# The layer norm's negated mean on VectorE instead of GpSimd, in a fused window-attention kernel

## What is computed

```
def ln(x, g, b):
    m = jnp.mean(x, -1, keepdims=True)
    v = jnp.mean(jnp.square(x - m), -1, keepdims=True)
    return (x - m) * jax.lax.rsqrt(v + LN_EPS) * g + b
...
q = ln(q.reshape(B_, E, L).transpose(0, 2, 1), gq, bq)     # k and v alike
attn = jax.nn.softmax(jnp.einsum('bhqd,bhkd->bhqk', q * SCALE, k) + bias[None], axis=-1)
out = jnp.einsum('bhqk,bhkd->bhqd', attn, v)
```

## Time and profile before

| | |
|---|---|
| Median of 3 runs | 852.89 us (851.65 to 853.03) |
| The profiled execution | 853.24 us, its span 851.1 us, 2.1 us outside the span |
| Mean granted clock of TensorE | 0.984 |
| Busy: TensorE / VectorE / ScalarE / GpSimd | 761.1 / 660.4 / 605.7 / 483.2 us |
| Group norm and weights, before the first head | 0 to about 35 us |
| Attention part of one image with its head | about 155 us |
| From one image to the next | about 204 us |

### The profile page before, as it was taken

How to read it: one execution, slowest core, us unless ns; L and a number is a source line. 1 busy time by engine, 2 the same in 40 slices (tenths; PEclk the granted TensorE clock), 3 DMA queues, 4 the chain that set the end, 5 groups by cost and what they waited for, 6 DMA issues and landing times.

```text
span 851.1 us, 19126 instructions
## 1 busy us (share of the span) xinstructions
PE 761.1 (89%) x5704; PEld 537.6 (63%) x5704; DVE 660.4 (78%) x2142; ACT 605.7 (71%) x1287; POOL 483.2 (57%) x1041
## 2 busy tenths in 40 slices
PE   0479999999788999999888999999989899999988
PEld 0347777766356777767445777776735677777753
DVE  6558888878657888878675888887866788888575
ACT  1498888765478888876457888877556888886651
POOL 5468677752237777764144776776233677776410
PEclk9999999999999999999999999999999999999999
DMA  7110123000231030300052013110014212000004
GB/s 250 56 29 30 48 108 106 1 1 1 87 125 55 28 128 0 106 1 2 1 166 70 29 30 126 52 55 1 1 56 137 64 34 78 0 1 2 1 1 148
DMA packets 17655, 47.14 MB, mean 55 GB/s; under 512 B 2080, under 2 KB 2720, under 8 KB 17568
## 3 DMA queue, kind: packets, MB, share of 16 engines
q1 hardware_dynamic: 17568, 46.09, 16.6%
HBM read 37.69 MB, written 8.39 MB: 54 GB/s over the span
## 4 chain that ended last, share of the span: by engine, by line
PE 44%; issue 19%; DVE 16%; POOL 11%; ACT 8%; DVEq 1%; DMA 0%; SPq 0%; ACTq 0%; POOLq 0%
PE y_ps L998 12%; PE o_ps L1065 7%; PE pt_ps L1055 5%; PE s_ps L1044 5%; POOL ln_rs L715 4%; PE s_ps L1087 4%; DVE ln_st L540 3%; ACT qk_n L840 3%; PE ox_ps L1014 3%; PE y_ps L969 2%; ACT sc L855 2%; PE t_ps L1023 2%; ACT v_bd L848 2%; DVE h_hi L509 2%; PE y_ps L993 1%
## 5 line engine op out<-in xcount | busy, mean ns | idle before, releaser
L840 ACT ACTIVATE qk_n<-y_ps,ln_nr,ln_rs 128x128 f32<-128x128 f32 x256 | 103.5, 456 | 81.8 <-POOL ln_nr L718 81.1
L998 PE MATMUL y_ps<-w_hi,x_hi 128*128 128x192 f16 (+1 forms) x512 | 149.9, 293 | 0.0
L998 PE MATMUL y_ps<-w_hi,x_lo 128*128 128x192 f16 (+1 forms) x512 | 149.5, 292 | 0.0
L998 PE MATMUL y_ps<-w_lo,x_hi 128*128 128x192 f16 (+1 forms) x512 | 149.5, 292 | 0.0
L728 POOL TENSOR_TENSOR sc<-sc,mx 128x512 f32<-128x512 f32 x128 | 133.7, 1045 | 22.0 <-DVE mx L566 21.5
L1065 PE MATMUL o_ps<-v_bd,pt 128*128 128x66 f32 x1024 | 128.6, 268 | 0.0
L1065 PEld LDWEIGHTS o_ps<-v_bd,pt 128*128 128x128 f32 x1024 | 124.5, 192 | 0.2
L551 DVE TENSOR_TENSOR sc<-s_ps,biasS 128x512 f32<-128x512 f32 x128 | 86.5, 676 | 47.4 <-PE s_ps L1044 45.4
L540 DVE BATCH_NORM_STATS2 ln_st<-y_ps 128x6 f32<-128x128 f32 x384 | 88.7, 286 | 42.6 <-PE y_ps L998 35.5
L715 POOL TENSOR_TENSOR ln_rs<-ln_ve,neg_half 128x3 f32<-128x3 f32 x128 | 113.0, 883 | 10.7
L711 POOL TENSOR_TENSOR ln_ve<-ln_mv,eps_y 128x3 f32<-128x3 f32 x128 | 24.8, 194 | 154.1 <-DVE ln_mv L545 153.8
(11 more groups left out here) (161 smaller groups left out, 1636.5 us busy)
## 6 DMA issues: line engine op xcount, KB each, us to landing
xs<-in_x_sh_dram SPq DMA_DIRECT2D x32, 576.0 KB, 3.9
xst<-in_x_al_dram SPq DMA_DIRECT2D x16, 512.0 KB, 6.8
xf<-in_x_al_dram SPq DMA_DIRECT2D x32, 256.0 KB, 4.2
out_dram<-xf SPq DMA_DIRECT2D x32, 256.0 KB, 2.4
wst<-in_wqkv_dram SPq DMA_DIRECT2D x1, 768.0 KB, 3.8
w1s<-in_w_dram SPq DMA_DIRECT2D x1, 256.0 KB, 8.7
w2s<-in_w_dram SPq DMA_DIRECT2D x1, 256.0 KB, 8.7
biasS<-in_bias_t_dram SPq DMA_DIRECT2D x1, 256.0 KB, 9.4
```

The costliest lines, as they stand in the source:

```text
L840: ins = act.activation(qk_n[j][:, t, :].rearrange("p (h y x) -> p h y x", h=HEADS, y=2), by_head(y_ps[j][:, E * t:E * (t + 1)]), ACT.Identity,
L998: ins = pe.matmul(y.rearrange("p (t e) -> p t e", t=3)[:, :, cols], xx[r % 2][:, s, a % 2, 2 * TS * (a // 2):2 * TS * (a // 2 + TS)], ww[: ...
```

## The change

GpSimd no longer computes `ln_nm`; VectorE does, behind the aggregation, after a wait on its own `ln_moments`. A new semaphore `ln_negated` tells GpSimd that `ln_nm` is there, and GpSimd waits for it between `ln_rs` and `ln_nr`. `ln_var_eps` is now added to by `ln_ve`. Shapes, values and buffers stay.

```
--- before.py
+++ after.py
@@ -544,6 +545,9 @@
                     for t in range(3):
                         ins = v.bn_aggr(ln_mv[m % 2][:, t, :], ln_st[m % 2][:, t, :])
                     ins.then_inc(ln_moments, 1)
+                    v.wait_ge(ln_moments, p0 + (m + 1))
+                    v.tensor_scalar(ln_nm[m % 2][:, :], ln_mv[m % 2][:, :, 0], -1.0, None, ALU.mult).then_inc(
+                        ln_negated, 1)
                 if has(i):
                     v.wait_ge(scores_done, p0 + (i + 1))
                     if i >= 4:
@@ -708,13 +712,13 @@
                     pool.wait_ge(ln_moments, p0 + (m + 1))
                     if m >= 2:
                         pool.wait_ge(ln_v, p0 + (m - 1))
-                    pool.tensor_tensor(ln_ve[j][:, :], ln_mv[j][:, :, 1], eps_y[:, :], ALU.add)
-                    pool.tensor_scalar(ln_nm[j][:, :], ln_mv[j][:, :, 0], -1.0, None, ALU.mult).then_inc(
+                    pool.tensor_tensor(ln_ve[j][:, :], ln_mv[j][:, :, 1], eps_y[:, :], ALU.add).then_inc(
                         ln_var_eps, 1)
                     pool.wait_ge(ln_var_eps, p0 + (m + 1))
                     pool.tensor_tensor(ln_rs[j][:, :], ln_ve[j][:, :], neg_half[:, 0:3], ALU.pow).then_inc(
                         ln_pow, 1)
                     pool.wait_ge(ln_pow, p0 + (m + 1))
+                    pool.wait_ge(ln_negated, p0 + (m + 1))
                     pool.tensor_tensor(ln_nr[j][:, :], ln_nm[j][:, :], ln_rs[j][:, :], ALU.mult).then_inc(
                         ln_scales, 1)
                     pool.tensor_tensor(ln_vs[j][:, 0, :], vec[:, WIN0:WIN1 + 1],
```

More of the change, by code:

```diff
@@ L204, in conv_attention @@
         ln_scales = sem("ln_scales")
+        ln_negated = sem("ln_negated")
         ln_v_scales = sem("ln_v_scales")
```

## The result

The changed kernel takes 844.06 us (median of 4 runs, 843.16 to 844.61) where the kernel before takes 852.70 (4 runs, 851.65 to 853.03): a ratio of 0.990, interval 0.9882 to 0.9917, so 8.6 us faster. The profiled execution took 843.50 us with a span of 841.5, against 853.24 and 851.1.

What follows compares the result with a forecast made beforehand. TensorE was taken as the bound, waiting for qk_n behind VectorE, GpSimd and ScalarE in series. 27 waits x 0.175 = 4.7 us off the 852.9 median gave 848.2 us, range 845.3 to 853.1.

Steps and rivals of the forecast that it cites:

- What bounds the kernel: Attention loop: TensorE is full except for short waits for qk_n, with VectorE, GpSimd and ScalarE late in series.
- GpSimd's part: GpSimd's ln_ve to ln_rs: dropping ln_nm shortens 0.49 to 0.27 us, saving 0.22 in each of 128 steps.
- The second wait: GpSimd before ln_nr: the satisfied wait on ln_negated costs 0 to 0.09 us, taken as 0.045, leaving 0.175 saved.
- the 27 places of the prediction: TensorE's 29 waits for qk_n at the transposes, counted as 27, each to shrink by 0.175 us.
- the heads: Start of each image: long TensorE waits for qk_n (2.79 us at 259.44); three of the first image's four share one saving.
- rival 3: Chain of waits: all 41 powers count, not 27, so 7.2 us saved, 845.7 us; chance 0.08.
- VectorE's part: VectorE behind the aggregation: ln_nm adds about 0.19 us per step where saturated, but costs the kernel nothing.
- 0.90, 0.55 and 0.59: Slack covering ln_nm on VectorE: idle before bias addition, wait before statistics, and softmax maximum's lead over GpSimd's subtraction, in us.
- Shared ports: VectorE and GpSimd contending for SBUF: ln_ve held by ln_nm would end no later than now, so nothing was charged.
- Rival 1: Shared ports make ln_ve start only after ln_nm ends; about 0.12 of 0.175 us is lost, 851.4 us; chance 0.20.
- rival 2: GpSimd's x_lo subtraction holds ln_nm through ln_ve and the power, one step of four; 3.6 us slower, 856.5; chance 0.12.
- The clock: One TensorE stretch at half clock may come or go when gaps in the heads shift: 1.7 us either way.

Runs made afterwards that it cites:

- e2: Kernel before without ln_nm anywhere: ln_nr made from the mean itself, minus sign missing, no second wait, nothing added on VectorE; 841.72 us, ratio 0.9865.
- e5: Kernel before with ln_nm still on GpSimd, but multiplying by a tile of -1 instead of a constant; 849.34 us, ratio 0.9948.
- e4: Kernel before with the negated mean computed twice on GpSimd, the first into a tile nobody reads; 862.07 us, ratio 1.0087.
- e7: Changed kernel with ln_nm on VectorE moved behind the bias addition in three steps of four; 841.77 us, ratio 0.9883.
- e1: Kernel before with VectorE also computing the negated mean into an unread tile, GpSimd unchanged; 854.06 us, ratio 1.0015.
- e6: Changed kernel with a second small dependent operation on VectorE behind ln_nm; 847.34 us, ratio 0.9941.
- e8: Changed kernel with variance plus epsilon also on VectorE, ahead of ln_nm, so GpSimd begins with the power; 841.92 us, ratio 0.9872.
- e9: Changed kernel with variance plus epsilon on VectorE too and ln_nm behind the bias addition in three steps of four; 840.30 us, ratio 0.9848.

## Why the prediction was too small, step by step

**What bounds the kernel.** Right in kind: the path ran through GpSimd's chain, and TensorE's wait was the place where most of that showed. Two steps of the sum failed: the size of one saving, and the number of places where it counts. The second goes back to the sentence "no more can be won in a row of the loop than its one short wait".

**GpSimd's part.** The 0.22 came as worked out (0.491 to 0.271). The second wait, which I put at 0.045 between ends of 0 and 0.09, costs 0 (e2 and the kernel after, both 0.927). And the power became 0.034 shorter, which no row of the kernel before could show, since there every power follows the same instruction (e5 shows it). The chain is therefore 0.255 shorter and not 0.175, beyond the prediction's end of 0.22 too. This step, the saving per place, was mis-sized by 0.08: with the 27 places of the prediction, 2.2 us, the larger half of the miss.

**The places.** This is the other step that failed. I counted TensorE's listed waits for qk_n: outside the heads four short ones and one of 0.99 in each image, 20 in all. What the runs show are seven stretches in each image that are one chain shorter: the five rows between pairs 8 and 28, the pairs from 28 to 31, and the stretch from pair 31 to the next image. Five of them hold a listed wait, and in e2 that wait shrinks by what the stretch gains (0.25 to 0.26). Two hold none: the row from pair 8 to 12, and the pairs from 28 to 31. In the latter there is a wait of the projection for its copy, kernel before and kernel after:

```profile
375.95 1.12 PE L1014 MATMUL ox_ps<-ot,projg 128*128 128x512 f32 x2 [0.51 <-ACT ot L827]
```

```profile
371.41 1.13 PE L1018 MATMUL ox_ps<-ot,projg 128*128 128x512 f32 x2 [0.39 <-ACT ot L831]
```

That is 0.12 of it. Laying TensorE's matmuls of the kernel before and of e2 on each other one by one gives the rest: e2 gets ahead by 0.10 and 0.04 at the transposes of the exponentials (pt_ps, 368.11 and 372.19 in the kernel before) and by 0.13 at the projection. In the row from pair 8 to 12 it gets ahead by 0.07 and 0.09 at pt_ps (273.63 and 277.90) and by 0.04 and 0.05 at t_ps (276.76 and 276.92), with no wait for qk_n listed at any of them. The loads of the transposes' weights show why at 368.11, kernel before and e2 (at 277.90 alike, 0.25 there and 0.16 in e2):

```profile
368.10 0.42 PEld L1055 LDWEIGHTS pt_ps<-idf,sc 128*128 128x128 f32 x4 [0.22 <-ACT sc L855]
```

```profile
362.85 0.42 PEld L1054 LDWEIGHTS pt_ps<-idf,sc 128*128 128x128 f32 x4
```

They waited for the exponential, which ScalarE does behind the norm; in e2 no such wait is marked. So GpSimd's chain reaches TensorE by at least three ways: qk_n, the exponential, and the copy for the projection. What ended the delays of 0.04 to 0.07 at the other places the rows don't mark. Counted by stretches, GpSimd's part is worth 27 x 0.255 = 6.9 outside the heads (27, since the last image has no next one), and e2 shows 5.32 + 1.58 and 0.27 in the last image, 7.2. The chain of waits had the number ready: 41 powers, which was rival 3's, and which e2, e4 and e5 bear out (45, 45 and 37 for each microsecond; 39, 42 and 38 without the clock). 41 x 0.255 less VectorE's 2.3 is 8.2 of the 8.6 measured. I had given it 0.08, because I couldn't name the waits behind the other 14.

**VectorE's part.** I costed it at nothing, with 0.90, 0.55 and 0.59 as its cover. Not nothing: 2.3 us within the change by the medians (e7 and e2 against the change), 0.9 alone (e1, 0.1 to 2.4 by its interval); without the clock's part 1.3 to 1.7, and 1.5 for e1. The sums in the second column put 0.6 of it in the loop: -4.70 against -5.32, in the rows that gained 0.19 instead of 0.26. The rest lies in the first rows of the images, which I hadn't followed ("could only follow in one period"); that it does is what is left over, and no run shows it by itself. The wait for the statistics was to shrink from 0.55 to 0.2 and is gone; its total fell by 27 us.

**Shared ports.** Right for ln_ve: it costs nothing. Ln_ve starts at 306.79, 0.17 after the aggregation as before, and ends 306.98 - 306.62 = 0.36 after it, in the 0.26 to 0.36 of the prediction, though ln_nm was running at 306.66 to 306.83. At 318.98 it starts 0.08 after the aggregation, with ln_nm still running for 0.13 us, and takes its usual 0.19. In the loop it starts 0.16 after the aggregation for two pairs of four and 0.08 for the other two, before, after and in e2 alike, and no ln_ve of the kernel after takes over 0.20. Rival 1 is refuted by this. By the Trainium skill's sentence (SBUF — State Buffer, Who interferes with whom) that the other engine fully blocks, the ln_ve of 318.98 would have had to wait for ln_nm's end at 319.11 and end 0.19 later, at 319.30, if ln_nm ran in a two-port mode; it ended at 319.17. So the trace doesn't bear out the use that I made of the rule; that there is a block, in the other direction, the rows of rival 2 show.

**Rival 2** is refuted for the loop, where it was priced: ln_nm takes 0.17 us in every step of it, and the bias addition after the subtraction for x_lo still has idle time ahead of it (0.66 at 319.76 in the kernel after, 0.90 before). But its mechanism exists. VectorE and GpSimd of the kernel after, in the first image:

```profile
59.19 0.65 DVE L549 TENSOR_SCALAR ln_nm<-ln_mv 128x3 f32<-128x3 f32 x1
```

```profile
58.66 1.16 POOL L697 TENSOR_TENSOR x_lo<-xnf,x_hi 128x512 f16<-128x512 f32 x1
```

The subtraction for x_lo had begun before ln_nm and ended at 59.82; ln_nm, 0.17 us elsewhere, ended 0.02 later. In this trace five of 128 are held like that (0.20 to 0.65 us), all for pairs 5 and 6 of an image, so in the first rows, where the rest of VectorE's cost is to be sought. In e1 the operation takes 0.77 once and 0.50 to 0.55 three times in the same rows, and in e6 the ln_nm of pair 30 takes 1.04 us in each image, held by the subtraction for xr_lo. Behind the power it is not held: in e7 ln_nm runs inside it and takes 0.16. So in these traces it is GpSimd's operations on 512 columns that hold it, to their end, and being held "through ln_ve and the power" did not come.

**The heads.** Seven long waits, 1.2 us. Pairs 0 to 8 show -2.83; without the two pieces at half clock (2 x 0.85) that is -1.1. That the two agree means little: the same column has -4.52 in e2 and -6.04 in e7, and the clock is mixed with all of them.

**The clock.** One piece of TensorE at half clock was priced at 1.7 us, and measures at most 0.85. That such pieces come and go was there (eight to six in the profiled pair), at half the size for each; that it is the shifted gaps that move them no run shows, and the same kernel twice has eight and seven.

**The sum as it came out** for the profiled pair, -9.7 us: 7.2 from the chain outside the heads, less 0.7 that VectorE's part cost there (6.5 measured: 4.70 + 1.49 + 0.27); 1.1 in the first two rows of the images; 1.7 from the clock; some 0.4 ahead of the first image's rows, after the last and outside the span. (How the 2.8 of the first two rows divide between clock and chain hangs on the 0.85.) For the medians, with 0.5 from the clock instead of 1.7, it is 8.5, and 8.6 was measured. Of the 3.9 us that the forecast missed, 2.2 are the size of one saving (27 x 0.08) and 1.8 the seven places that it left out (7 x 0.255); 0.5 is the clock and 0.4 the ends; VectorE's part outside the heads took back 0.7, and the heads gave 0.7 less than their seven places at 0.255. That is 3.5, within 0.4 of what was measured.

## What to carry to other kernels

Where a chain of small operations runs once per step beside a full engine, its weight is better taken from the chain of waits (its share, divided by the length of one; 41 here) than from the number of waits that the full engine shows (27): delays in series come out at several places, as gaps before other work. When work moves to an engine with some slack, its place in that queue decides: a small operation that waits for its own engine's last result costs more than its length if it stands before work that others wait for, and less if it stands behind it (e7, 2.3 us). And lengthening the same chain by one operation (e4) is a cheap way to learn what shortening it will bring: 45 us for each us of chain in e4, 45 in e2.

## What was not expected of the hardware

- GpSimd's power on 128x3 elements takes 0.881 to 0.883 us behind a multiplication by a constant and 0.849 to 0.851 behind an operation on two tensors (128 of each in every kernel; in e8 and e9, where it comes first in the step, 0.851).
- GpSimd's multiplication by a constant, 128x3, takes 0.239 us (0.228 for the second of two in e4), the one by a second tensor 0.192.
- A second wait, already satisfied, ahead of a GpSimd operation added nothing that the records show (0.927 from the power to ln_nr with and without).
- A VectorE multiplication by a constant on 128x3 (0.17 us) that begins while GpSimd is in an operation on 128x512 ends 0.02 us after it, up to 1.04 us long (e6); inside GpSimd's power on 128x3 it takes 0.16 (e7). A GpSimd addition of two tensors on 128x3 that begins while it runs is not lengthened (0.19).
- On VectorE the second of two small operations after one wait starts 0.08 us after the first (e8: 306.35, 306.43), where one that waits for the other's result starts 0.20 after it (e6). E6's pair:

```profile
304.96 0.17 DVE L550 TENSOR_SCALAR ln_nm<-ln_mv 128x3 f32<-128x3 f32 x1
305.16 0.17 DVE L553 TENSOR_SCALAR ln_nx<-ln_nm 128x3 f32<-128x3 f32 x1
```
